# A first tile loaded and computed in another order, and expert weights split in 512-column pieces with one pause each

## The reference

```python
# 1: cross attention, 16 heads of 16, context of 257 rows of 192 per sequence
q, k, v = ln(x) @ Wq, context @ Wk, context @ Wv
x = x + softmax(where(mask, q @ k.T * hd ** -0.5, max_neg)) @ v @ Wo
# 2: local attention, a window of 5 rows, with biases
x = x + local_attention(ln(x), Wq, bq, Wk, bk, Wv, bv)
# 3: mixture of 8 experts, the best one for each token
for e in range(8):
    h = gelu(ln_x @ W1[e] + b1[e])        # 256 -> 1024
    h = gelu(h @ W2[e] + b2[e])           # 1024 -> 512
    out += expert_mask[:, e:e+1] * (h @ W3[e] + b3[e])   # 512 -> 256
x = x + out
```

## Time and profile before

| | |
|---|---|
| median of three runs | 791.76 us |
| the profiled execution | 792.73 us, its span 791.0 us |
| PE busy | 716.1 us (91% of the span) |
| DVE busy | 474.5 us (60%) |
| ACT busy | 453.0 us (57%) |
| POOL busy | 433.4 us (55%) |
| mean granted TensorE clock | 0.976 |

### The profile page before, as it was taken

How to read it: one execution, slowest core, us unless ns; L and a number is a source line. 1 busy time by engine, 2 the same in 40 slices (tenths; PEclk the granted TensorE clock), 3 DMA queues, 4 the chain that set the end, 5 groups by cost and what they waited for, 6 DMA issues and landing times.

```text
span 791.0 us, 26602 instructions
## 1 busy us (share of the span) xinstructions
PE 716.1 (91%) x9191; PEld 608.5 (77%) x9192; DVE 474.5 (60%) x1389; ACT 453.0 (57%) x1070; POOL 433.4 (55%) x566
## 2 busy tenths in 40 slices
PE   4799999999999999999999674999999999997995
PEld 3688788888888888888888573787888788875874
DVE  1455666676667666766677638998952990288000
ACT  2556566666666666666666205656657557563752
POOL 6356555555555555555554411577576776674543
PEclk9899999999999999999999996999999999999998
DMA  5322222322332233333322801229124422271000
GB/s 168 88 80 75 75 74 86 86 73 73 86 86 73 73 86 86 72 74 86 86 73 88 320 28 50 80 85 324 41 94 156 135 100 85 85 243 32 20 7 1
DMA packets 55007, 73.85 MB, mean 93 GB/s; under 512 B 5839, under 2 KB 40688, under 8 KB 54962
## 3 DMA queue, kind: packets, MB, share of 16 engines
q1 hardware_dynamic: 49716, 60.96, 25.8%
q0 software_dynamic: 2944, 8.13, 3.4%
q10 hardware_dynamic: 2304, 4.20, 1.4%
HBM read 66.91 MB, written 7.27 MB: 94 GB/s over the span
## 4 chain that ended last, share of the span: by engine, by line
PE 67%; DVE 10%; issue 10%; POOL 4%; DMA 3%; ACT 3%; SPq 1%; POOLq 1%; DVEq 0%; ACTq 0%
PE ps_s L1459 14%; PE ps_kv L1181 8%; PE ps_p L1220 5%; PE ps_kv L1173 5%; PE ps_o L1206 4%; PE ps_s L1192 4%; PE ps_p L1411 3%; PE ps_o L1479 3%; PE ps_kv L1411 3%; DVE w L1158 3%; DVE w L1155 3%; PE ps_m L1316 2%; PE ps_m L1312 2%; PE ps_m L1270 2%; PE ps_s L1443 2%
## 5 line engine op out<-in xcount | busy, mean ns | idle before, releaser
L725 ACT ACTIVATE prob<-prob,neg_max 128x257 f32<-128x257 f32 x256 | 112.8, 501 | 68.6 <-DVE neg_max L912 68.5
L912 DVE CUSTOM_DVE_ANT_0 prob<-ps_s,mask_add 128x257 f32<-128x257 f32 x256 | 95.5, 420 | 50.7 <-PE ps_s L1192 50.5
L1155 DVE CAST w<-w_raw 128x512 fp32r<-128x512 f32 (+1 forms) x108 | 68.2, 632 | 66.8 <-DMA w_raw<-in_L_ffn_W_dram 60.4
L1158 DVE TENSOR_TENSOR w<-w_raw,w 128x512 fp32r<-128x512 f32 (+1 forms) x128 | 102.8, 803 | 5.1 <-DVE w L1158 0.9
L1459 PE MATMUL ps_s<-w,h_hi 128*128 x368 | 93.9, 406 | 12.5 <-DVEq L1161 7.0
L568 POOL TENSOR_TENSOR ctx_parts<-ctx_raw,ctx_parts 128x512 fp32r<-128x512 f32 x64 | 82.3, 1286 | 37.6 <-ACT ctx_parts L720 37.4
L1173 PE MATMUL ps_kv<-ctx_parts,wkv_hi 128*128 128x256 f32 x512 | 86.7, 297 | 10.3 <-DVE wkv_hi L1025 10.3
L1459 PEld LDWEIGHTS ps_s<-w,h_hi 128*128 128x128 f32 x368 | 68.6, 190 | 32.4 <-issue 17.8
L1181 PE MATMUL ps_kv<-wkv_hi,ctx_parts 128*128 128x256 f32 x512 | 87.1, 299 | 2.7 <-ACT kT L729 0.3
L1220 PE MATMUL ps_p<-ident,prob 128*128 128x128 f32 x512 | 80.1, 277 | 0.9 <-DVE probT L934 0.8
L1173 PEld LDWEIGHTS ps_kv<-ctx_parts,wkv_hi 128*128 128x128 f32 x512 | 71.4, 191 | 11.7 <-issue 10.3
(11 more groups left out here) (198 smaller groups left out, 1523.9 us busy)
## 6 DMA issues: line engine op xcount, KB each, us to landing
w_raw<-in_L_ffn_W_dram SPq DMA_DIRECT2D x24, 1024.0 KB, 7.9
ctx_raw<-in_ctx_turned_dram SPq DMA_DIRECT2D x64, 256.0 KB, 3.4
mask_add<-mask_dram SPq DMA_DIRECT2D x64, 128.5 KB, 3.3
rows_dram<-x3n ACTq DMA_DIRECT2D x16, 256.0 KB, 3.7
w_raw<-in_L_ffn_W_dram SPq DMA_DIRECT2D x8, 512.0 KB
xt<-in_x_dram SPq DMA_DIRECT2D x16, 128.0 KB, 2.6
xr<-in_x_dram SPq DMA_DIRECT2D x16, 128.0 KB, 2.3
slot_x<-rows_dram,slot_ids POOLq DMA_INDIRECT x23, 3.7
```

The source lines that it names most:

```text
L725: a.activation(prob[:, g, :], prob[:, g, :], ACT.Exp, bias=neg_max[:, g:g + 1], scale=-1.0).then_inc(exp_done, 1)
L912: d.tensor_tensor_reduce(prob[:, r, :], ps_s[r][:, 0:J], mask_add[:, k, :], -(HD ** -0.5), 3.0e38, ALU.add, ALU.min, neg_max[:, r:r + 1]). ...
L1155: d.tensor_copy(w[:, b, HI, part], raw[:, b, part]).then_inc(rounded, 1)
L1158: d.tensor_tensor(w[:, b, LO, part], raw[:, b, part], f32(w[:, b, HI, part]), ALU.subtract).then_inc(rounded, 1)
```

## The change

Three things change.

First, the first tile. The mask bytes, the last context rows, the first context and Wq are issued by ACT instead of SP. SP's order becomes x, Wk, the store of the mask, Wv, a context, the first mask, the second tile of x, and the rest behind it. The mask rows are made by DVE. Wk and Wv are split separately, with semaphores of their own. `iteration(-1)` on PE becomes `keep_clock(16)`, the transposes of x, `keep_clock(10)`, the queries, `keep_clock(3)`, the keys and `keep_clock(4)`; the values of batch 0 and the product with the last context rows (`last_rows`) move behind `scores` of batch 0. POOL places the queries of batch 0 before it prepares the second context. The four selects that make `band` (L525) move on POOL from the start to the end of `iteration(0)`.

Second, the expert weights: a piece of 1024 columns (W3) is taken in 512 instead of 256 columns; behind a TENSOR_TENSOR DVE no longer waits, except for the pieces rounded early, and the last one reports the piece itself.

Third, `keep_clock(20)` becomes `keep_clock(34)`.

```diff
+            sp.dma_start(wkv[:, 0, 0, :], Wk[0:P, :]).then_inc(k_in, 16)
...
             sp.wait_ge(mask_done, 1)
             sp.dma_start(mask_dram, mask_rows[:, :]).then_inc(mask_stored, 16)
+            sp.dma_start(wkv[:, 1, 0, :], Wv[0:P, :]).then_inc(v_in, 16)
...
+            load_ctx(0, 1)
+            sp.wait_ge(mask_stored, 16)
+            load_mask(0, 0)
+            sp.wait_ge(xn1_done, 1)
+            load_x(xt, 1, x_in)
+            load_ctx(0, 2)
+            for b in range(1, BT):
+                load_mask(0, b)
+            load_ctx(0, 3)
             for dst, w in ((wo, Wo), (wr, Wr)):
...
                 if isinstance(T, int) and T == 0:
+                    prepare_band()
                     prepare_routing()
...
+                    act.dma_start(mask_bytes[:, :], mask).then_inc(mask_bytes_in, 16)
+                    act.dma_start(last_ctxT[:, :, :], last_turned.rearrange("(c p) b -> p c b", p=P)).then_inc(last_in, 16)
+                    act.dma_start(ctx_raw[:, 0, :, :], ctx_turned[0].rearrange("(c p) j -> p c j", p=P)).then_inc(ctx_in[0], 16)
+                    act.wait_ge(consts, 1)
+                    a.activation(row_inv[:, 0:1], neg_half[:, :], ACT.Exp, bias=neg_half[:, 0:1])
+                    act.dma_start(wq[:, :, :], Wq.rearrange("(c p) n -> p c n", p=P)).then_inc(wq_in, 16)
+                    act.wait_ge(k_in, 16 * 3)
+                    a.copy(wkv_hi[:, 0, :, :], wkv[:, 0, :, :]).then_inc(wk_rounded, 1)
                     round_ctx(0, 0)
+                    middle(T, 1)
+                    act.wait_ge(v_in, 16 * 3)
+                    a.copy(wkv_hi[:, 1, :, :], wkv[:, 1, :, :]).then_inc(wv_rounded, 1)
+                    copy_k(0)
                     round_ctx(0, 1)
                     copy_v(0, 0)
...
-                    quarter = (columns.stop - columns.start) // 4
-                    for at in range(columns.start, columns.stop, quarter):
-                        part = slice(at, at + quarter)
+                    for at in range(columns.start, columns.stop, 512):
+                        part = slice(at, at + 512)
                         if not early:
                             d.tensor_copy(w[:, b, HI, part], raw[:, b, part]).then_inc(rounded, 1)
                             k += 1
                             dve.wait_ge(rounded, k)
-                        d.tensor_tensor(w[:, b, LO, part], raw[:, b, part], f32(w[:, b, HI, part]), ALU.subtract).then_inc(rounded, 1)
-                        k += 1
-                        dve.wait_ge(rounded, k)
-                    dve.sem_inc(ready, 1)
+                        last = d.tensor_tensor(w[:, b, LO, part], raw[:, b, part], f32(w[:, b, HI, part]), ALU.subtract)
+                        if at + 512 == columns.stop:
+                            last.then_inc(ready, 1)
+                        elif early:
+                            last.then_inc(rounded, 1)
+                            k += 1
+                            dve.wait_ge(rounded, k)
...
+                    pe.wait_ge(consts, 3)
+                    keep_clock(16)
+                    middle(T, 0)
+                    keep_clock(10)
+                    middle(T, 1)
+                    keep_clock(3)
                     pe.wait_ge(consts, 6)
+                    pe.wait_ge(wk_split, 2)
                     keys(0, 0)
+                    keep_clock(4)
                     return
...
                     if in_tiles(T):
                         scores(n, k)
+                    if isinstance(T, int) and T == 0 and k == 0:
+                        pe.wait_ge(wv_split, 2)
+                        values(0, 0)
+                        last_rows()
...
-            keep_clock(20)
+            keep_clock(34)
```

More of the change, by code:

```diff
@@ L440, in ahead @@
             def ahead(T):
-                sp.wait_ge(xn1_done, T)
-                load_x(xt, T, x_in)
+                if not (isinstance(T, int) and T == 1):
+                    sp.wait_ge(xn1_done, T)
+                    load_x(xt, T, x_in)
                 if not (isinstance(T, int) and T < 3):
@@ L531, in _, with prepare_band @@
                 g.memset(v[:, buffer, :, :, HD:BLOCK], 1.0).then_inc(consts, 1)
-            pool.wait_ge(zeroed, n + 1)
+            pool.wait_ge(zeroed, 6)
             g.tensor_tensor(head_mask[:, :], head_parity[:, 0:HP], head_parity[:, HP:HG], ALU.add).then_inc(consts, 1)
+            def prepare_band():
+                n = 6
+                for base, mult, pattern in ((2, 1, [[-1, P]]), (2, -1, [[1, P]]),
+                                            (0, 1, [[-S, BT], [0, S]]), (S - 1, -1, [[S, BT], [0, S]])):
+                    view = band[:, :] if len(pattern) == 1 else band[:, :].rearrange("p (a b) -> p a b", b=S)
+                    g.affine_select(out=view, in_=view, compare_op=ALU.is_ge, fill=MASKED, base=base,
+                                    pattern=pattern, channel_multiplier=mult).then_inc(zeroed, 1)
+                    n += 1
+                    pool.wait_ge(zeroed, n)
             def prepare_routing():
@@ L596, in iteration @@
                     split_ctx(0, 0)
-                    pool.wait_ge(mask_bytes_in, 16)
-                    g.tensor_scalar(mask_rows[:, :], mask_bytes[:, :], 1.0, -MASKED, ALU.subtract, ALU.mult).then_inc(mask_done, 1)
+                    pool.wait_ge(m_emptied, turn(T, 2) + 1)
+                    place_queries(0)
                     shift_ctx(0, 1)
+                    scale_of(0, 1)
                     split_ctx(0, 1)
+                    for b in range(1, BT):
+                        place_queries(b)
                     shift_ctx(0, 2)
+                    return
                 for k in range(BT):
                     n = BT * T + k
-                    if k == 0 and has_q and in_tiles(T):
+                    if k == 0 and has_q and not (isinstance(T, int) and T == 0):
                         scale_of(0, T + 1)
@@ L889, in last_rows @@
             def last_rows():
-                dve.wait_ge(consts, 6)
                 dve.wait_ge(last_step, 1)
@@ L1248, in middle @@
                     my_turn(T, 2)
+                    if isinstance(T, int) and T < 0:
+                        pe.wait_ge(wq_in, 16)
                     if has_q:
@@ L1336, in iteration @@
                 if first:
+                    pe.wait_ge(consts, 3)
[4 more added lines that the diff above has]
+                    keep_clock(3)
                     pe.wait_ge(consts, 6)
-                    pe.wait_ge(kv_in, 16 * 6)
-                    pe.wait_ge(wkv_split, 3)
+                    pe.wait_ge(wk_split, 2)
                     keys(0, 0)
-                    middle(T, 0)
-                    values(0, 0)
-                    middle(T, 1)
-                    last_rows()
+                    keep_clock(4)
                     return
-                if isinstance(T, int) and T == 0:
-                    pe.wait_ge(last_copied, 1)
                 for k in range(BT):
@@ L1352, in iteration @@
                         scores(n, k)
+                    if isinstance(T, int) and T == 0 and k == 0:
+                        pe.wait_ge(wv_split, 2)
+                        values(0, 0)
+                        last_rows()
+                    if isinstance(T, int) and T == 0 and k == 1:
+                        pe.wait_ge(last_copied, 1)
                     if not first and exists(T, k - 1) and not (isinstance(T, int) and BT * T + k > B):
```

55 lines of the change are left out of this document (23 added, 32 removed).

## The result

The changed kernel takes 781.47 us (median of four runs, 781.06 to 781.93), the kernel before 792.67 in the same series (four runs, 791.49 to 794.66). The ratio is 0.9848, 95% interval 0.9828 to 0.9869: faster by 11.2 us. The forecast was 774.5 with a range of 771.2 to 780.0, so the direction was right and the gain came out a third smaller than the 17.3 summed. The profiled execution of after took 781.61, its span is 779.8, the mean granted clock 0.970 (before 0.976).

What follows compares the result with a forecast made beforehand. PE, busy 716.1 of 791.0 us, was taken as the bound, so gains come from its idle or half-clock time: 11.8 - 1.1 + 2.3 + 1.0 + 3.3 = 17.3, median 774.5, range 771.2 to 780.0.

Steps and rivals of the forecast that it cites:

- The start: First tile: first mask at about 12.4 us, second at 19.3 instead of 31.13; gain 11.8, bounds 10 and 12.6.
- The rival that it would gain only 8: First tile: PE at half clock, slow loads, exponentials held; second mask at 23, gain 8, time 778.3; chance 0.15.
- The band: Selects at the end of `iteration(0)` make POOL's rstd for tile 2 late; loss 1.1, bounds 0 and 1.7.
- keep_clock(34): Ahead of the slots: fourteen more transposes hold the full clock for the first matmuls; gain 2.3, bounds 0 and 2.6.
- The bound of "nothing": Lower bound for the added clock transposes ahead of the slots: the clock falls anyway, gain 0.
- Expert 2: DVE's W2 splitting gets shorter without pauses; gain 1.0 of PE's 1.15 us stall.
- The chain of experts 6 and 7: DVE's splits of W2, W3 and the next W2 shorten by 1.1, 1.2 and 1.0; gain 3.3, all on the path.
- rival (d): Experts: without pauses POOL's operations wait for DVE, 35 us over 16 slots, slower by 18; chance 0.04.
- (a): Expert weights: pauses are free, only W3 shortens the chain, 0.8; sum 13.8, time 778.0; chance 0.13.
- (c): More than the sum: clock stays up behind expert 7 (1.3), start at its bound (0.8); 772.4; chance 0.11.
- The sum: All terms of the whole kernel: 11.8 - 1.1 + 2.3 + 1.0 + 3.3 = 17.3 us gained, median 774.5.

Runs made afterwards that it cites:

- band_late_only: The kernel before with only the four band selects moved to the end of `iteration(0)`: 795.53 us, ratio 1.0016.
- start_only: The changed kernel with the old weight pieces and `keep_clock(20)`, so only first tile and band changed: 786.91 us, ratio 0.991.
- clock34_only: The kernel before with `keep_clock(34)` for `keep_clock(20)` and nothing else: 795.68 us, ratio 1.0026.
- band_at_start: The changed kernel with the four band selects back at the start of POOL's work: 780.13 us, ratio 0.9831.
- spread_28: The changed kernel with band selects behind step 0 and routing constants behind step 2 of tile 0, 28 clock transposes for 34: 777.57 us, ratio 0.9796.
- x1_early: The kernel before with the load of x of tile 1 moved behind the first mask load: 788.5 us, ratio 0.9935.
- after_again: The changed kernel, unchanged, measured again in another series: 780.69 us, ratio 0.9838.

## Why the prediction was right and where it was wrong

**The start, forecast 11.8: right.** Measured 11.4 to batch 4 (48.41 to 37.03). First mask 12.41 (12.4 forecast), second 19.62 (19.3). `mask_rows` on DVE took 0.26 for the 0.4 taken. The rival that it would gain only 8 is refuted by these two marks. The path was not quite the one summed: the keys were to wait for the queries, with the split context ready at 8.3. The queries were through at 8.70, the split context (1.48 us of POOL from 7.59) only at 9.07, and it was this that the keys at 9.32 waited for. It came 0.8 later than taken and still fell inside the 8.8 to 9.8 taken for the queries: to that extent, some tenths of 11.8, the mark is right by luck.

**The band, forecast a loss of 1.1: the wait right, the clock left out.** `rstd` is late and DVE waits 0.99. At a granted clock of 1.00 on both sides the move costs 1.4 in the stretch of batch 5 (9.35 against 7.98), inside the bounds of 0 and 1.7. The profile gives 2.4, since after ran 6.6 us of this stretch at half clock, for which the forecast had no term: that is the other 1.1. The half clock is not the band's alone, as the five traces at 8.65 to 8.75 have it without the band there. (With the old start `band_late_only` took 9.02 at 0.81, against 8.65 to 8.73 at 0.80.)

**`keep_clock(34)`, forecast 2.3: right in its stretch, in part by luck.** 10.78 to 8.53 is 2.25 (the terms listed for it give 2.2). But `start_only` has 8.52 with 20 transposes, as one of the two traces with the new start and 20: the gain can come without the 34, which made it come every time. Besides, two terms that I took as independent are not: with the old pieces this gain runs into DVE's splitting for expert 2 (1.4 given back in `clock34_only`, with the delay of the transposes; 4.8 in `start_only`, half clock included). In after, where the pieces changed too, PE does not wait there. The bound of "nothing" that I set below it was too mild: the kernel with this change alone came out 0.26% slower, by a cause that is open in part.

**Expert 2, forecast 1.0:** the stall of 1.15 is gone (0 in after, 1.03 in `band_at_start`, which has the same pieces); the stretch shows 0.7.

**The chain of experts 6 and 7, forecast 3.3: this is the term that was mis-sized.** It measured 2.2. The step said that the 3.3 were "all of it on the path". Without the time lost beside POOL the chain fell from 23.27 to 19.64 (chain less lost, before and after), by 3.6, even a little more than forecast: 0.12 per pause, and W3's half. But the lost time rose from 9.2 to 10.6. In the five kernels with the old pieces it is 9.1 to 9.4, with the pauses and W3 in 512 it is 9.66, and in seven of the eight traces without pauses it is 10.55 to 10.89; `spread_28` has 9.88. POOL has the same operations to do in it. I priced the pause as empty time. In part it was the time in which a POOL operation went by that now meets one of DVE's. That the loss grows with the pauses gone is shown by the seven of eight; that the pause itself let POOL by is my reading of it. The rule of the Trainium skill that the port pair of DVE and GpSimd is an exclusive lock (SBUF — State Buffer, section "Who interferes with whom") agrees with the rows: DVE's 0.69 becomes 1.66 beside `h_lo`, and ends after it. My rival (d) had this mechanism with the wrong victim: POOL did not starve, DVE paid, and 1.4 us in place of 35.

**Rivals (a) and (c).** That the pauses are free (778.0) is refuted by 31.80 against 30.22, though its time would have been nearer the 781.47 than the forecast was. That the clock stays up behind expert 7 (1.3) did not come: the stall stayed at 3.27 and eight products took 3.77.

**The sum.** Of the 6.1 us missing between 17.3 and 11.2, the chain is 1.1, batch 5 1.3, expert 2 0.3, the start 0.4. The other 3.0 are in stretches that the sum put at nothing, without a reason given: batches 5 to 9 0.35, the loop 0.64, the last batch to the routing 0.96, the tail 0.96. The loop belongs to the edit, by the way the traces sort: 355.7 to 356.2 in all nine traces with the new start and 355.99 in `x1_early`, against 355.0 to 355.4 in the four others, some 0.05 us per tile. Batches 5 to 9 go with it: where no half clock falls into them they take 27.15 to 27.22 with the new start, 26.85 to 26.87 with the old. What the ten share is the early load of x of tile 1; how it lengthens the later tiles I did not find. Ahead of the routing the traces with the new start lie between 35.23 and 36.35 (mean 35.8), the others between 35.07 and 35.68 (mean 35.4) with before the lowest, so by these means less than half of that 0.96 is the edit's. The tail falls on either 64.7 to 65.0 or 65.6 to 65.8 with old and new code alike, by how long the half clock lasts, and is not. The profiled execution of before was a short one in batch 5 and ahead of the routing, and a sum made against it inherits that. So of the 6.1 about 2.0 are half clock that lasted longer in this trace of after than in that of before (1.1 in batch 5, 1.0 in the tail), and `after_again` is shorter by just these two; what the clock did in the executions that were not profiled is not known. In the repeated series the gain was 13.1 (793.83 to 780.69), still 4 short. So two steps failed: the pauses priced as empty time (3.3 for 2.2), and every stretch outside the edited places taken as unchanged, where about 3 us were given back. The second is why the range ended at 780.0. How much of it is the edit's and how much the clock's differs from trace to trace, and for the loop the cause is open.

## What to carry to other kernels

Price a shortened stall together with the next one: gains that let PE arrive earlier are paid out only if the engine it then waits for was shortened too, and a longer stall can cost twice, by the half clock behind it (4.8 us in `start_only` for a stall 1.6 longer). When pauses are taken out of a chain on DVE that runs beside POOL's operations, do not count on all of the empty time: here 3.6 us of it gave 2.2. Before building a new order for a start, move the one load that ends last on the chain: it was worth 6.1 of 11.4 us here. And compare a stretch only with traces that had the same granted clock in it.

## What the runs showed of the hardware

- The stretches at half clock come and go between executions of one kernel: 6.6 us at 0.50 in one, at 0.82 in the other; 3.3 us at 0.50 in one, at 1.00 in the other. They also last on while PE is full, as at 716.5 to 719.8 (3.30 of 3.30 busy). That is 1 us each, and 2.5 us of span.
- A block that is to keep the clock up has no fixed length: 34 transposes took 5.68 us in one kernel and 6.48 in another, and the longer one held up the work that it was to serve. 28 were enough in the one trace taken and had 0.65 us to spare, and 20 were enough in one trace of six.
- A pause of DVE for its own semaphore costs 0.12 us between operations of 512 columns: pairs of 1.19 against 1.07.
- A DVE operation of 0.43 or 0.69 us that meets a POOL TENSOR_TENSOR takes up to 1.54 or 1.72 in after, on 13 meetings in 30 us.
